# An attention stage whose small VectorE steps, second ending and matrix work are put in another order

## The reference

```python
_, top_idx = jax.lax.top_k(query_norms, top_u)          # 409 of 2048, per batch and head
Q_sel = jnp.take_along_axis(Q, top_idx[:, :, None], axis=1)
scores = jnp.einsum('bud,bld->bul', Q_sel, K) * scale
attn = jax.nn.softmax(scores, axis=-1)
out_sel = jnp.einsum('bul,bld->bud', attn, V)           # scattered back to the rows of top_idx
```

## Time and profile before

| what | value |
|---|---|
| median of 3 runs | 1130.31 us (1128.67 to 1131.53) |
| the profiled execution's own time | 1130.18 us |
| its span | 1128.4 us |
| busy in the span: PE, DVE, ACT, POOL | 80%, 78%, 53%, 51% |
| attend, first score matmul to last `finish` | about 225.9 to 556.4 us |

### The profile page before, as it was taken

How to read it: one execution, slowest core, us unless ns; L and a number is a source line. 1 busy time by engine, 2 the same in 40 slices (tenths; PEclk the granted TensorE clock), 3 DMA queues, 4 the chain that set the end, 5 groups by cost and what they waited for, 6 DMA issues and landing times. The chain is left out here.

```text
span 1128.4 us, 26554 instructions
## 1 busy us (share of the span) xinstructions
PE 908.3 (80%) x7725; PEld 567.7 (50%) x7726; DVE 876.8 (78%) x2069; ACT 596.5 (53%) x1351; POOL 579.4 (51%) x595
## 2 busy tenths in 40 slices
PE   7999300269999999999767741899999999999995
PEld 4444100212232323232246631777778888888894
DVE  4795688798999999998368877577777777777774
ACT  2565185217888887878534423454544444444441
POOL 2353383343767676763498930245454444545443
PEclk9999655558999999999879865899999999999998
DMA  7234773110111111120269921999952323323232
GB/s 242 104 134 146 241 229 96 42 27 22 29 33 26 36 24 38 24 79 4 70 189 248 268 70 10 254 225 226 224 105 46 53 42 51 47 47 51 42 48 29
DMA packets 125020, 110.55 MB, mean 98 GB/s; under 512 B 17488, under 2 KB 114448, under 8 KB 124944
## 3 DMA queue, kind: packets, MB, share of 16 engines
q1 hardware_dynamic: 102816, 86.76, 25.6%
q0 software_dynamic: 20480, 21.53, 11.9%
q10 hardware_dynamic: 1648, 1.31, 0.4%
HBM read 50.98 MB, written 35.50 MB: 77 GB/s over the span
## 5 line engine op out<-in xcount | busy, mean ns | idle before, releaser
L988 DVE TENSOR_REDUCE attend_mxh<-attend_p_a 128x1 f32<-128x512 f32 x416 | 255.4, 683 | 6.8 <-PE attend_p_a L1156 5.3
L1083 ACT ACTIVATE w<-attend_p_b 128x409 f32<-128x409 f32 x512 | 227.1, 518 | 50.9 <-PE attend_p_b L1171 50.7
L1898 ACT ACTIVATE expert_hr<-expert_p,b1t 128x256 f32<-128x256 f32 (+1 forms) x376 | 134.4, 423 | 193.1 <-PE expert_p L1836 169.7
L1791 POOL DMA_INDIRECT out_x<-expert_ys,expert_drop x72 | 120.3, 1671 | 194.6 <-DVE expert_ys L1933 137.7
L1858 PE MATMUL expert_p<-w,expert_hhi 128*128 x800 | 136.6, 273 | 0.5 <-DVE expert_ys L1933 0.2
L1836 PE MATMUL expert_p<-expert_xhi,w 128*128 128x256 f16 x800 | 136.4, 273 | 0.0
L913 POOL DMA_INDIRECT attend_qsel<-q_d,idx x96 | 91.5, 953 | 72.4 <-DVE attend_mxh L988 55.3
L1171 PE MATMUL attend_p_b<-attend_qb,w 64*128 64x409 f16 x512 | 114.5, 345 | 12.1 <-ACT w L1083 11.2
L1183 PE MATMUL attend_p_o<-w,attend_vh 128*32 128x409 f32 x1024 | 115.5, 524 | 0.0
L928 POOL DMA_INDIRECT attn_d<-outs,idx x90 | 89.7, 997 | 44.2 <-DVE otail L1019 15.2
L1781 POOL DMA_INDIRECT expert_xs<-h_d,expert_take x72 | 72.5, 1007 | 74.7 <-DVE expert_take L1937 53.7
(11 more groups left out here) (350 smaller groups left out, 1756.4 us busy)
## 6 DMA issues: line engine op xcount, KB each, us to landing
expert_wu<-w SPq DMA_DIRECT2D x88, 256.0 KB
w<-in_L_ffn_w SPq DMA_DIRECT2D x20, 512.0 KB, 4.5
q_d<-project_q SPq DMA_DIRECT2D x32, 256.0 KB, 2.0
x<-in_L_attn_x SPq DMA_DIRECT2D x8, 512.0 KB, 10.8
attn_d<-zero SPq DMA_DIRECT2D x8, 512.0 KB
w<-k_d SPq DMA_DIRECT2D x32, 128.0 KB
route_ain<-attn_d SPq DMA_DIRECT2D x32, 128.0 KB, 3.3
route_xin<-in_L_attn_x SPq DMA_DIRECT2D x32, 128.0 KB, 2.8
```

The costliest lines, as they stand in the source:

```text
L988: dve.tensor_reduce(mxh[:, h, c, k:k + 1], p_a[chunk_use(q, a, h) % 4][:, :], AX, ALU.max).then_inc(a_done, 1)
L1083: act.activation(prob[:, 2 * (j % (TPB // 2)) + h, :], p_b[tile_use(p, j, h) % 3][:, 0:TOP], ACT.Exp, scale=SCALE / UNIT ** 2).then_inc(pr ...
L1791: pool.indirect_dma_start(out=out, out_offset=bass.IndirectOffsetOnAxis(ap=drop[u][:, s:s + 1], axis=0), in_=ys[u][:, s, :], in_offset=Non ...
L1898: last = act.activation(hr[g % 2][:, f, rows], p_1[g][:, f, rows], ACT.Relu, bias=cst["b1t"][:, bass.ds(e[s] * FB + 2 * g + f, 1)], scale= ...
```

## The change

The instructions stay the same but for one more memset; their order changes, and `mxh` has two buffers.

- VectorE: the three copies stand before maximum 19 of their own pair (26 maxima, counted from 0); the reduction before maximum 0 of the next pair, the high part before its maximum 1, the low part before its maximum 2. The ending's reciprocals (now `divisors`) stand before maximum 14 and the multiplications (`finish`) before maximum 15, where they stood before maximum 8. The chunk of the last queries comes as chunk 8 and not as chunk 12. In each chunk the head of partitions 64 to 127 comes first.
- PE: a chunk stands behind both tiles of a key block. Four chunks of pair p + 2 stand in pair p's loop instead of three. Values are placed anew.
- ScalarE: `products` behind tile (1, 0), `queries` behind (10, 0), `queries_max` behind (14, 1).
- POOL: each gather and scatter waits for two more maxima.

```diff
-        TURN_AT = 9
+        TURN_AT, TAIL_AT = 12, 8
+        def rows_and_keys(a):
+            return (FULL, 0) if a == TAIL_AT else divmod(a - (a > TAIL_AT), NK)
-            return 1 + USES_A * q + 2 * a + h + (1 if a >= TURN_AT else 0)
+            return 1 + USES_A * q + 2 * a + (1 - h) + (1 if a >= TURN_AT else 0)
-                    wait(pool, a_done, min(CHP * (p + 1) + 6 + 2 * at, CHP * NP))
+                    wait(pool, a_done, min(CHP * (p + 1) + 8 + 2 * at, CHP * NP))
...
-                for a in range(NA):
-                    maxima(0, a)
-                minus_maximum(0)
-                for a in range(3):
-                    maxima(1, a)
-                for p in range(NP):
-                    maxima(p + 1, 3)
-                    if p > 0:
-                        finish(p - 1)
-                    for a in range(4, NA):
-                        maxima(p + 1, a)
-                    if p + 1 < NP:
-                        minus_maximum(p + 1)
-                    for a in range(3):
-                        maxima(p + 2, a)
+                for q in range(NP):
+                    for s in range(CHP):
+                        if q > 0 and s == 0:
+                            minus_maximum(q - 1)
+                        if q > 0 and s == 1:
+                            high(q - 1)
+                        if q > 0 and s == 2:
+                            low(q - 1)
+                        if q > 1 and s == 14:
+                            divisors(q - 2)
+                        if q > 1 and s == 15:
+                            finish(q - 2)
+                        if s == 2 * TAIL_AT + 3:
+                            move_tails(q)
+                        maximum(q, s // 2, 1 - s % 2)
...
+                def scores(p, j, ahead=0, a=0, between=None):
+                    for h in range(2):
+                        scores_tile(p, j, h)
+                    if between:
+                        between()
+                    if ahead and p + ahead < NP:
+                        chunks(p + ahead, a)
...
                 for p in range(NP):
+                    scores(p, 0, 1, 4)
+                    scores(p, 1, 1, 5, (lambda: values(p - 1, 7)) if p > 0 else None)
+                    scores(p, 2, 1, 6)
                     if p > 0:
                         results(p - 1)
+                    scores(p, 3, 1, 7)
+                    scores(p, 4, 1, 8)
+                    scores(p, 5)
                     values(p, 0)
+                    scores(p, 6, 1, 9)
+                    scores(p, 7, 1, 10, lambda: values(p, 1))
+                    scores(p, 8)
                     values(p, 2)
+                    scores(p, 9, 1, 11)
                     turn_q(p + 2)
+                    scores(p, 10, 1, 12)
                     values(p, 3)
+                    scores(p, 11, 2, 0)
+                    scores(p, 12, 2, 1, lambda: values(p, 4))
+                    scores(p, 13)
                     values(p, 5)
+                    scores(p, 14, 2, 2)
                     turn_m(p + 1)
+                    scores(p, 15, 2, 3)
                     values(p, 6)
```

More of the change, by code:

```diff
@@ L801, in attend_block @@
         pvs = sb("pvs", [P, TOP], F32)
-        mxh = sb("mxh", [P, 2, QT, NK], F32)
+        mxh = [sb(f"mxh{i}", [P, 2, QT, NK], F32) for i in range(2)]
         mneg = sb("mneg", [P, 2, QT], F32)
@@ L841, in wait_chunk_bank @@
         def wait_chunk_bank(pe, use):
-            before = use - 4
+            before = use - CB
             if before < 0:
@@ L985, in maximum @@
                 def maximum(q, a, h):
[L986 to L993, removed]
+                    c, k = rows_and_keys(a)
+                    dve.wait_ge(a_ps, CHP * q + 2 * a + (1 - h) + 1)
@@ new lines, in high, with low @@
+                def high(q):
+                    wait(dve, mq_ps, q)
+                    dve.wait_ge(v_step, VSTEP * q + 2)
+                    dve.tensor_scalar(mpart[:, :, :, 0], mneg[:, :, :], 1.0 / STEP_M, None, ALU.mult).then_inc(v_step, 1)
+                def low(q):
+                    dve.wait_ge(v_step, VSTEP * q + 3)
+                    dve.scalar_tensor_tensor(out=mpart[:, :, :, 1], in0=mneg[:, :, :], scalar=1.0 / STEP_M, in1=mpart[:, :, :, 0], op0=ALU.mult, op1=ALU.subtract).then_inc(v_step, 1)
@@ L1036, in _ @@
                     if p == 0:
-                        dve.memset(mxh[:, :, :, :], -3e38).then_inc(zero_done, 1)
+                        for m in mxh:
+                            dve.memset(m[:, :, :, :], -3e38).then_inc(zero_done, 1)
                         dve.memset(mpart[:, :, :, :], 0.0).then_inc(zero_done, 1)
@@ L1150, in scores_chunk @@
                         pe.wait_ge(k_here[q % KB], 64 * (q // KB + 1))
-                    for h in range(2):
[L1152 to L1172, removed]
+                    use = chunk_use(q, a, h)
@@ new lines, in scores_chunk @@
+                    wait_chunk_bank(pe, use)
+                    into, rows = p_a[use % CB], slice(HP * h, HP * h + HP)
+                    if c < FULL:
+                        last = pe.matmul(into[:, :], qa[q % 2][rows, c * P:(c + 1) * P], kt[q % KB][rows, k * CH:(k + 1) * CH], start=True, stop=True, tile_position=(HP * h, 0))
+                    else:
+                        for w in range(NK):
+                            last = pe.matmul(into[32 * w:32 * w + QTAIL, :], qa[q % 2][rows, c * P:TOP], kt[q % KB][rows, w * CH:(w + 1) * CH],
+                                             start=True, stop=True, tile_position=(HP * h, 32 * w))
@@ new lines, in scores_chunk, with scores_tile @@
+                    last.then_inc(a_ps, 1)
+                def scores_tile(p, j, h):
+                    if j == 0 and h == 0:
+                        pe.wait_ge(mq_done, p + 1)
+                    use = tile_use(p, j, h)
+                    wait_tile_bank(pe, use)
+                    rows = slice(HP * h, HP * h + HP)
+                    pe.matmul(p_b[use % TB][:, 0:TOP], kt[p % KB][rows, j * P:(j + 1) * P], qb[p % 2][rows, 0:TOP],
+                              start=True, stop=True, tile_position=(HP * h, 0)).then_inc(b_ps, 1)
```

129 lines of the change are left out of this document (53 added, 76 removed).

## The result

| | before | after |
|---|---|---|
| median | 1129.49 us (1128.28 to 1131.53, 4 runs) | 1144.98 us (1142.98 to 1149.12, 4 runs) |
| profiled execution, its span | 1130.18, 1128.4 | 1149.12, 1147.3 |
| attend, from the first memset of its block to the end of `finish` | 213.6 to 556.4: 342.8 | 215.9 to 574.6: 358.7 |
| first tile of pair 1 to first tile of pair 15 | 264.2 | 274.8 |

The ratio is 1.0138 (1.0118 to 1.0159). The change makes the kernel slower by 15.5 us; the forecast was 1128.6, 0.9 less than before. After's profile is of the longest of its four executions, so its parts add up to more than the medians' 15.5: of the 18.9 us between the spans 15.9 lie in attend, 2.3 in the blocks ahead of it, which the change doesn't touch, and 0.7 behind.

The account below looks back on a forecast made before the run. VectorE looked like the present bound; afterwards a ring over PE and VectorE, 18.75 us a pair against 18.89. From 1130.18: -2.0 over 14 pairs, +0.8 start, -0.5 end, so 1128.5, as median 1128.6; range 1122 to 1134.5.

Parts of the forecast that it names:

- the first term of the change on VectorE: VectorE's three partition-moving copies: they stay at 0.17 us each and add 0.52 us (0.5 to 0.65) to a pair's maxima.
- POOL's turns: POOL's later gathers and scatters in attend: they cost nothing, as scatters wait for out_done and queries were done a pair earlier.
- chunk 12's wait: On PE, between V0 and chunk 5: chunk 12 with a short wait for its bank, 0.31 us a pair.
- a sign of being wrong: On PE: waits for VectorE's maxima at chunks other than 12 would show the forecast wrong.
- The ring: PE and VectorE: V0 (values(p, 0)) to chunk 5, 14.60 us, then maxima and ending to next V0, 4.15: 18.75 a pair.
- V0 does not wait: Faster rival, chance 0.18: PE's own row sets the pair, 14.60 + 3.7 = 18.3 us, 1122.7 with the ends.
- The new neighbours: Slower rival on PE: chunks beside tiles of the same partitions cost 0.87 us a pair, 1140.8; chance 0.15 with other stalls.
- Small steps overlap: On VectorE: steps without a wait for the one just before start 0.10 us apart; maxima overlap by 0.08.
- The ends: First and last pairs of attend: start +0.8 us (0 to 2), pair 14 -0.5 (-0.7 to 0), pair 15 17.1 against 17.0.
- The clock: TensorE's granted clock in the blocks behind attend: could move the time either way; chance 0.06, no size given.
- K: Later theory, not in the prediction: PE's pause before V0 makes the clock fall, for 3.4 us in some pairs.
- T: Later theory, not in the prediction: new places of values slow the last pair through a clock fall, 23.2 us against 20.4.

Follow-up runs that it names:

- g0: The changed kernel with its three copies written as one-element reductions, on an undisturbed chip: 1137.82 us, ratio 1.0056 to the kernel before.
- j0: The kernel of i1 with the three reductions before maximum 24 instead of 19: 1127.91 us against 1130.04 for the kernel before, ratio 0.9983.
- e0: The unchanged kernel after, on a disturbed chip: ratio 1.0002 to the kernel before.
- f1: The unchanged kernel after, on another disturbed chip: ratio 1.0012 to the kernel before.
- i1: The changed kernel with reductions for copies, reciprocals and multiplications one maximum earlier, and the last pair's values and results at old places: 1131.56 us, ratio 1.0001.
- h4: The kernel before with only finish moved behind two more maxima, on a disturbed chip: 1216.8 us against 1203.5, ratio 1.0152.
- e1: The changed kernel with POOL's copy of V (spread_v) ahead of the gathers, on a disturbed chip: 1208.2 us against 1197.9, ratio 1.0068.

## Why the prediction was wrong

- **The step that failed** is the first term of the change on VectorE: "the three copies move partitions; they stay at their 0.17 each, as in rows 3 ... 0.52 (0.5 to 0.65)". Measured: 0.67, 0.64 and 0.08 to the next start, 1.4 us, and 1.5 with the overlap that is lost ahead of them (401.14 to 405.05 for four maxima and the copies, less 4 x 0.598). In g0, where nothing is held, the same sum gives 0.52. The rows showed copies only at the end of a pair, beside scatters; the change put them before maximum 19, beside POOL's last gather and its COPY. The forecast said of POOL's turns that they cost nothing, and never laid POOL's timeline beside the new place. The three runs above show the holding by taking away each side of it and by making it in the kernel before.
- **It was on the path.** By the forecast VectorE had 1.5 us of a pair to spare, but not at this place. It kept chunk 12's wait short ("0.31", with the maxima in time). In after chunk 12 waits 0.51, and chunk 11, where any such wait was named as a sign of being wrong, 0.26; the way from V0 to V3 is 0.82 longer than in g0.
- **The holding is not all of the miss.** It is about 9 of the 15.5 us. Without it g0 takes 1137.8, still above the forecast's 1134.5. What is left is the clock inside attend, for which the forecast had no term, and the start.
- **The ring was right, its gain was not there.** Without the holding, in g0: V0 to chunk 5 14.80 (forecast 14.60), chunk 5 to V0 4.07 and 4.18 in turn (4.15), a pair 18.92 (18.75). V0 waited for `otail`, VectorE idled 0.59 before maximum 10, `turn_m` waited for nothing. But a pair of the kernel before takes 18.87 in the mean of the 14, so the 2.0 us that the ring should have saved are none. The term that is too small is chunk 12: with its tile pair it takes 0.88 (381.20 to 382.08 in g0's weight loads), where the forecast has 0.28 + 0.31.
- **"V0 does not wait" was priced right** as a rival: 3.7 from chunk 5 to V0 measures 3.70 in j0, the pair 18.48 against 18.3, the difference again about that of chunk 12. The forecast had 1122.7 for it; j0's median is 1127.9, with 6.0 of the expected 7.9 us in the 14 pairs of its profile. (The 7.9 doesn't follow exactly from its own terms: 18.89 less 18.3 is 0.59 a pair, 8.3 us.)
- **The new neighbours cost nothing.** A tile pair with its chunk takes 0.49 in the new order too (384.95 to 385.44 in g0's weight loads), as in the earlier trace rows, and g0's pair leaves no room for 0.87.
- **Small steps overlap**, as the earlier trace rows said. The Trainium skill, "VectorE: DVE Perf Modes", section "The DRAIN you can't avoid", says that chaining steps without semaphores saves nothing; the 0.07 to 0.11 above contradict it here, and agree with its own pointer to the section on steps with no wait between them.
- **The ends** were missed: to the first tile +0.95 and the first pair +1.3, together 2.3 for the forecast's 0.8. The clock rose at 266.5 us, before at 260.1, where the forecast held it to rise at the same time. 2.3 us of the 6.4 lie in the blocks ahead. Pair 14 had -0.5 and gave -0.1. The last pair had +0.1 and cost +3.0; in after, 6.8 us of it are at half clock from 556.7.
- **The clock** had 0.06 in the chances, and for the blocks behind only. It fell inside attend in after and g0, in the middle and at the end.

The cause of the held copies has a rule in the Trainium skill, "SBUF — State Buffer", section "Who interferes with whom": VectorE and GpSimd share a pair of ports, which the one that comes first keeps for a whole instruction; copies can ask for it, a reduction on trn2 never does. The runs agree in the main: copies 0.16 to 0.67, reductions never above 0.15. They don't show that the pair is kept to the end of POOL's instruction: four copies that began 0.50 to 0.52 us into POOL's COPY of 0.62 took 0.16 (e0 and f1). By that rule the copies should have been priced from the gather's 0.95 and the COPY's 0.62; the forecast did not use it.

**What stays open.** K is supported and not shown. For it: of the profiles from undisturbed chips the two in which V0 waits for `otail` have two and three falls in the middle of attend, each at a V0, and the three in which it doesn't wait (before, i1, j0) have none. Against it as the only cause: most of these waits are followed by no fall, and on disturbed chips the clock falls in every kernel. It is one profile of each kernel, and i1 and j0 changed more than that wait. T holds in one half: the last pair is longer through the clock, and hardly through its places. Whether the places bring the fall isn't settled: with the new ones the clock falls in the last pair in 7 of 8 profiles, with the old ones in 4 of 8. The price of the holding was not shown in the kernel before, and rests on the comparison of after and g0 across two chips and on the pairs in their profiles.

## What to carry to other kernels

When a step is moved on one engine, lay the timeline of every other engine beside its new place, POOL's above all: a 0.16 us copy of 25 x 2 numbers became 0.66 there. A small VectorE move that must stand beside POOL's work can be written as a reduction over one element. And an ending that is put later is paid by whatever waits for the bank it frees: two maxima later cost 0.9 to 1.3 us a pair in h4. One maximum earlier, 0.60, gave back about 0.2 in i1 (18.92 to 18.73), since the next wait then set the pair. Last, a cause that is found and shown can still leave a part of the loss: set the kernel without it against the kernel before too.

## What was not expected of the hardware

- A copy can be held by an indirect DMA issue of POOL, not only by its COPY: 0.40 and 0.42 us beside a lone gather (e1), and 0.33 to 0.41 beside lone scatters in six pairs of h4. All of these began 0.51 to 0.60 us into the DMA's 0.95 and ended with it; those that began 0.07 to 0.49 into one without a COPY behind it took 0.16. In the kernel before copies stand at the start of scatters at 0.16 to 0.23.
- The granted clock fell to 0.50 for 3.4 us in single pairs, each time within 0.2 us of a V0, though most pairs have the same wait and V0 and no fall, and the pair took 1.1 to 1.3 us longer (g0).
- The same kernel takes 1130 us on some chips and 1198 to 1206 us on others, with idle moments common to VectorE and ScalarE and with 8 to 11 falls of the granted clock in 240 us. A change that cost 1.4% on the first kind measured 0.0% and 0.1% on the second.
